# A two-layer kernel with a GRU scan: input and constant loads by need, one gate product in front of the last weight turn, and the recurrence with its routing and output two steps sooner in the loop

## What is computed

```
proj  = attention over 8 block sums of x (keys Wk, query cond, softmax) through Wo
x     = x + FFN(layernorm(x + proj) * gamma + beta)          # layer 0
        FFN: silu(gate) * up, then down; 512 -> 2048 -> 512,
        activations and weights quantised in blocks of 32 (shared exponent)
h_t   = GRU(h_{t-1}, x_t), h_0 = cond, t = 0 .. 255           # layer 1
        r = sigmoid(i_r + h_r); z = sigmoid(i_z + h_z)
        n = tanh(i_n + r * h_n); h_t = (1 - z) * n + z * h_{t-1}
route = silu(h @ rw1.T + rb1) @ rw2.T + rb2 + gates           # top 2 of 16 experts
x     = x + h @ W.T + bias + sum over the 2 experts of rank-16 products
```

## Time and profile before

| | before |
|---|---|
| time, median of 3 runs | 1708.49 us (1707.1 to 1712.42) |
| the profiled execution's own time | 1712.84 us |
| its span | 1711.0 us |
| PE, PEld busy | 1551.7 us (91%), 1198.1 us (70%) |
| DVE, ACT, POOL busy | 1399.7 us (82%), 644.3 us (38%), 496.8 us (29%) |
| mean granted PE clock | 0.963 |
| first and last start of the r and n products | 226.87 us, 1691.36 us |

### The profile page before, as it was taken

How to read it: one execution, slowest core, us unless ns; L and a number is a source line. 1 busy time by engine, 2 the same in 40 slices (tenths; PEclk the granted TensorE clock), 3 DMA queues, 4 the chain that set the end, 5 groups by cost and what they waited for, 6 DMA issues and landing times.

```text
span 1711.0 us, 75109 instructions
## 1 busy us (share of the span) xinstructions
PE 1551.7 (91%) x32268; PEld 1198.1 (70%) x32268; DVE 1399.7 (82%) x5571; ACT 644.3 (38%) x1624; POOL 496.8 (29%) x573
## 2 busy tenths in 40 slices
PE   5633689999999999999999999999999999999986
PEld 2321367777777777777777777777777777778874
DVE  7787888888888888888888888888888888887654
ACT  5666243333333333333333333333333333333331
POOL 6774322222222222222222222222222222221000
PEclk9866699999999999999999999999999999999998
DMA  7744211112211111122111112212111212211000
GB/s 245 267 154 135 57 45 43 42 47 49 49 46 49 31 40 49 46 46 50 48 41 49 49 46 49 37 35 47 46 46 49 49 43 46 49 43 37 25 15 20
DMA packets 122444, 101.01 MB, mean 59 GB/s; under 512 B 91904, under 2 KB 92288, under 8 KB 121728
## 3 DMA queue, kind: packets, MB, share of 16 engines
q1 hardware_dynamic: 121824, 96.02, 21.1%
q10 hardware_dynamic: 288, 0.19, 0.0%
HBM read 58.43 MB, written 16.78 MB: 44 GB/s over the span
## 4 chain that ended last, share of the span: by engine, by line
PE 77%; DVE 14%; issue 3%; DMA 2%; POOL 2%; ACT 2%; SPq 0%; DVEq 0%; ACTq 0%; POOLq 0%
PE ps_rn_turn L1311 25%; PE ps_gi L1212 12%; PE ps_z L1311 10%; PE ps_down L1179 6%; PE ps_gate_up L1170 6%; PE ps_gate_up L1160 4%; PE ps_base L1221 4%; PE ps_base L1264 3%; PE ps_route L1221 3%; DVE fe L821 1%; POOL qfT L1028 1%; DVE gi L630 1%; DVE gi L628 1%; DVE hT L808 1%; PE ps_rn_turn L1200 1%
## 5 line engine op out<-in xcount | busy, mean ns | idle before, releaser
L1311 PEld LDWEIGHTS ps_rn_turn<-hT,whh 128*128 128x128 f16 x16320 | 435.0, 96 | 86.0 <-DVE hT L759 72.2
L1311 PE MATMUL ps_rn_turn<-hT,whh 128*128 128x32 f16 x16320 | 449.3, 177 | 46.1 <-DVE hT L759 45.4
L1046 POOL TENSOR_TENSOR qf<-f8c,fe 128x512 bf16<-128x512 bf16 x128 | 134.1, 1047 | 862.1 <-DVE f8c L838 862.1
L583 ACT ACTIVATE r_tanh<-r_pre,scale_half 128x64 f32<-128x64 f32 x256 | 89.0, 348 | 563.5 <-DVE r_pre L779 563.5
L1212 PEld LDWEIGHTS ps_gi<-x1T,wih 128*128 128x128 f16 x4608 | 270.6, 98 | 32.8 <-issue 3.1
L1212 PE MATMUL ps_gi<-x1T,wih 128*128 128x128 f16 x4608 | 289.3, 220 | 1.6 <-ACT gi L574 1.6
L1311 PE MATMUL ps_z<-hT,whh 128*128 128x32 f16 x8160 | 243.3, 177 | 0.0
L1311 PEld LDWEIGHTS ps_z<-hT,whh 128*128 128x128 f16 x8160 | 222.6, 96 | 0.0
L574 ACT ACTIVATE gi<-ps_gi,b_i,scale_x 128x128 f32<-128x128 f32 x384 | 144.4, 456 | 196.7 <-PE ps_gi L1212 196.7
L773 DVE TENSOR_TENSOR r_half<-ps_rn_turn,gi 128x64 f32<-128x64 f32 x256 | 57.2, 224 | 149.9 <-PE ps_rn_turn L1311 146.1
L585 ACT ACTIVATE z_tanh<-z_pre,scale_half 128x64 f32<-128x64 f32 x256 | 89.0, 348 | 157.0 <-DVE z_pre L789 157.0
(11 more groups left out here) (201 smaller groups left out, 2408.5 us busy)
## 6 DMA issues: line engine op xcount, KB each, us to landing
wih<-in_x_steps SPq DMA_DIRECT2D x32, 256.0 KB, 5.4
xin<-in_x_steps SPq DMA_DIRECT2D x32, 256.0 KB, 2.9
...
```

Of the source, the lines that this page charges most:

```text
L583: nc.scalar.activation(r_tanh[:, :], r_pre[:, :], ACT.Tanh, scale=HALF_S_INV).then_inc(r_ok, 1)
L1046: g.tensor_tensor(blocked(qf[:, :]), blocked(f8c[:, :]), spread(fe16[:, :]), ALU.mult).then_inc(qf_done, 1)
L1311: last = mm(ps[:, (at + j) * 2 * B:(at + j + 1) * 2 * B], whh[:, k, u, gate * D + j * P:gate * D + (j + 1) * P], hx(t)[:, 2 * k:2 * k + 2, ...
```

## The change

- **x and constants.** Block sums take 8 tiles in piece 0 and the rest over the next 9 (`sums_upto`; `SUM_PARTS` 10, so that hops and slots come two pieces sooner: `FIRST_HOP` 9, `FIRST_SLOT` 19). SP issues x one piece ahead of its sums, the first 8 tiles behind two weight pieces. The four constants of the attention come at pieces 7 and 8, the others at 14 to 18. The slots of c = -4 stand beside pieces 19 to 23, the last four of them before piece 23.
- **Gate product.** PE's `gate(0, 0)` is issued in front of the turn of piece 23; DVE's first `scales` in front of a constant's cast; the sum of the biases moves from an attention hop to `gru_weights`.
- **Two steps sooner** (`AHEAD`). R and L no longer go by s but by b: tile r and step b are those of c * 8 + s + 2. What was done in slot s for b = s now stands two slots sooner: b = 0 in slot 6 and 1 in slot 7 of the iteration before, b = 2 to 7 in slots 0 to 5. The loads of x1 and the stores of y go with them. Q, F, E and I stay where they were. `x_parts` end one slot sooner, ACT's `gi` moves from slots 1, 3, 5 to 1, 2, 4, and the `base` parts spread over b = 0, 1, 2, 6.

```diff
 XRING = 8
-SUM_PARTS = 12
+SUM_PARTS = 10
 ATTENTION = 10
 FIRST_HOP = SUM_PARTS - 1
 FIRST_SLOT = FIRST_HOP + ATTENTION
...
-FILL_UPS = 11
+FILL_UPS = 10
+AHEAD = 2
...
+def beside_piece(p):
+    if p < PIECES - 1:
+        return range(max(p - FIRST_SLOT, 0), max(p - FIRST_SLOT + 1, 0))
+    return range(p - FIRST_SLOT, STEPS)
+def sums_upto(p):
+    return 0 if p < 0 else min(TILES, XRING + p * (TILES - XRING) // (SUM_PARTS - 1))
...
-    return tuple(0 <= c + d < TILES for d in (4, 3, 2, 1, 0, -1))
+    return tuple(0 <= c + d < TILES for d in (4, 3, 2, 1))
+def recurrent(c, s):
+    r, b = divmod(c * STEPS + s + AHEAD, STEPS)
+    return r, b, 0 <= r < TILES, 0 <= r - 1 < TILES
...
-        if p < 0:
-            return 0
-        return min(TILES, max(min(p + 1, 2) * XRING // 2, (p - 1) * TILES // SUM_PARTS))
+        return sums_upto(p - 1)
...
-        if 8 <= p < 8 + (CONSTS + 1) // 2:
-            for dst, src in small[(p - 8) * 2:(p - 7) * 2]:
-                sp.dma_start(dst, src).then_inc(consts if p > 8 else att_consts, 16)
+        if p in (7, 8):
+            for dst, src in small[(p - 7) * 2:(p - 6) * 2]:
+                sp.dma_start(dst, src).then_inc(att_consts, 16)
+        if 14 <= p < 19:
+            for dst, src in small[(p - 12) * 2:(p - 11) * 2]:
+                sp.dma_start(dst, src).then_inc(consts, 16)
         if p == SUM_PARTS + 1:
             sp.dma_start(wk_sb, WkT).then_inc(wkwo_loaded, 16)
         if p == SUM_PARTS + 3:
...
         if 0 <= k < KD:
             sp.wait_ge(at_pe, 2)
             sp.dma_start(wih[:, k, :], W_hh[:, k, :]).then_inc(whh_loaded, 16)
-        if p >= FIRST_SLOT:
-            slot(-4, p - FIRST_SLOT)
+        for s in beside_piece(p):
+            slot(-4, s)
+    def load_x1(l):
+        wait(sp, x1b_done, count(l, 1))
+        sp.wait_ge(x1_stored, count(l, 1, 1) * 16)
+        sp.dma_start(x1_in[:, :], rows(x1_dram, l)).then_inc(x1in_loaded, 16)
+    def store_y(l):
+        sp.wait_ge(y_ok, count(l, 1, 1))
+        sp.dma_start(rows(out, l), y[:, :]).then_inc(y_stored, 16)
...
+        r, b, R, L = recurrent(c, s)
         turns(c, s)
         if s == 0:
             loads(c)
+        if L and b == 0:
+            load_x1(r - 1)
+        if L and b == STEPS - 1:
+            store_y(r - 1)
         if s == 4 and c + 5 < TILES:
...
-        if I and s in (1, 3, 5):
+        if I and s in (1, 2, 4):
...
-        if p >= PIECES - KD:
+        k = p - PIECES + KD + 1
+        if 0 <= k < KD:
             act.wait_ge(whh_loaded, 16 * KD)
-            absolute_sums(0, p - PIECES + KD, wih[:, p - PIECES + KD, :])
-    for s in range(STEPS):
-        slot(-4, s)
+            absolute_sums(0, k, wih[:, k, :])
     over_tiles(slot)
...
-            dve.wait_ge(consts, 16 * (CONSTS - 2))
-            v.tensor_tensor(b_i[:, 0:2 * KD], b_i[:, 0:2 * KD], b_h[:, 0:2 * KD], ALU.add).then_inc(c_dve, 1)
...
         if s == 3:
+            dve.wait_ge(consts, 16 * (CONSTS - 4))
+            v.tensor_tensor(b_i[:, 0:2 * KD], b_i[:, 0:2 * KD], b_h[:, 0:2 * KD], ALU.add).then_inc(c_dve, 1)
...
-        if L and here == (6, 0):
+        if L and there == (6, 0):
...
-            recur(c, s, beside)
+            recur(r, b, beside)
...
+    scales(0, 0)
     dve.wait_ge(first_consts, 32)
     v.tensor_copy(idb[:, :], idf[:, :]).then_inc(c_dve, 1)
-    scales(0, 0)
     scales(0, 1)
     scales(1, 0)
     for p in range(PIECES):
-        if p >= FIRST_SLOT:
-            slot(-4, p - FIRST_SLOT)
+        for s in beside_piece(p):
+            slot(-4, s)
...
+            if q == 0:
+                pool.wait_ge(consts, 16 * (CONSTS - 4))
...
-        if L and s == 3:
+        if L and b == 3:
...
-        for t in range(p * TILES // SUM_PARTS, min((p + 1) * TILES // SUM_PARTS, TILES)):
+        for t in range(sums_upto(p - 1), sums_upto(p)):
...
     def max_row(e, L):
         pe.wait_ge(x_small, count(e, 6, 2))
+        wait(pe, x_scale_ok, count(e, 1))
         if L:
-            pe.wait_ge(l_small, count(e - 3, 6, 1))
+            pe.wait_ge(wxaT_ok, count(e - 3, 1, 1))
...
-            pe.wait_ge(wxaT_ok, count(e - 3, 1, 1))
+            pe.wait_ge(xa_ok, count(e - 2, 1, 1))
...
-            wait(pe, x_scale_ok, count(l + 2, 1, 1))
+            wait(pe, x_small, count(l + 2, 6, 3))
...
+        pe.wait_ge(x_scale_ok, count(l + 2, 1, 1))
         turn_(ps_h1T, hid[:, :], idf[:, :]).then_inc(hidT_mm, 1)
...
-    def turn_wxa(l, E):
+    def turn_wxa(l):
         pe.wait_ge(wxa_ok, count(l, 1, 1))
-        if E:
-            pe.wait_ge(x_small, count(l + 3, 6, 3))
...
-    x_parts = ((0, (0,)), (0, (1, 2, 3)), (1, (0, 1)), (1, (2, 3)), (2, (0, 1)), (2, (2, 3)))
-    base_parts = {4: (0,), 6: (1, 2, 3)}
+    x_parts = ((0, (0, 1)), (0, (2, 3)), (1, (0, 1, 2, 3)), (2, (0, 1)), (2, (2, 3)))
+    base_parts = {0: (0,), 1: (1,), 2: (2,), 6: (3,)}
     base_parts_at_end = {0: (0,), 3: (1, 2, 3)}
...
-        if F:
+        if F and (f, s) != (0, 0):
             (gate, up)[s % 2](f, s // 2)
...
+        if (r, b) == (0, 0):
+            pe.wait_ge(inter_done, FILL_UPS)
         if R:
-            pe.wait_ge(hx_ok, c * STEPS + (s + 1))
-            t = c * STEPS + s - 1
+            pe.wait_ge(hx_ok, r * STEPS + (b + 1))
+            t = r * STEPS + b - 1
...
     for p in range(PIECES):
         block_sums(p)
         attention(p - FIRST_HOP)
+        if p == PIECES - 1:
+            pe.wait_ge(w_ev, PIECES - 1)
+            gate(0, 0)
         piece(p // 2, p % 2)
-    for s in range(STEPS):
-        slot(-4, s)
     pe.wait_ge(w_ev, PIECES)
```

More of the change, by code:

```diff
@@ L358, in beside @@
                     sp.dma_start(wih[:, k, :], W_hh[:, k, :]).then_inc(whh_loaded, 16)
-                if p >= FIRST_SLOT:
-                    slot(-4, p - FIRST_SLOT)
-            def loads(c):
[L363 to L367, removed]
+                for s in beside_piece(p):
[7 more added lines that the diff above has]
+                sp.dma_start(rows(out, l), y[:, :]).then_inc(y_stored, 16)
+            def loads(c):
+                Q, F, E, I = stages(c)
                 if E:
@@ L862, in ffn, with others @@
                         clip(f8c, f8, f8_done, at, qf_done, f8c_done)
-            def others(c, s, place, Q, F, E, I, L):
-                q, e, i, l = c + 4, c + 2, c + 1, c - 1
+            def others(c, s, place, Q, F, E, I, r, b, L):
+                q, e, i, l = c + 4, c + 2, c + 1, r - 1
                 ffn(c, s, place, F, E)
-                here = (s, place)
-                if L and here == (1, 0):
+                here, there = (s, place), (b, place)
+                if L and there == (1, 0):
                     dve.wait_ge(xa_ok, count(l, 1, 1))
@@ L886, in others @@
                     v.tensor_tensor(gap[:, :], top[:, 0:1], top[:, 1:2], ALU.subtract).then_inc(l_small, 1)
-                if L and here == (5, 2):
+                if L and there == (5, 2):
                     dve.wait_ge(l_small, count(l, 6, 5))
                     v.tensor_copy(at_f[:, :], top_at[:, :]).then_inc(l_small, 1)
-                if L and here == (6, 0):
+                if L and there == (6, 0):
                     dve.wait_ge(coeff_ok, count(l, 3, 3))
@@ L946, in others @@
                     clip(q8c, q8, q8_done, count(q, 1), qx_done, q8c_done)
-                if L and here == (7, 3):
+                if L and there == (7, 3):
                     dve.wait_ge(y_mm, count(l, 1, 1))
@@ L1062, in slot @@
                     g.tensor_tensor(x1_bias[:, :], x1_in[:, :], bias_b[:, :], ALU.add).then_inc(x1b_done, 1)
-                if L and s == 5:
+                if L and b == 5:
                     pool.wait_ge(gap_ok, count(l, 1, 1))
@@ L1084, in _ @@
                 piece(p // 2, p % 2)
-            for s in range(PIECES - FIRST_SLOT, STEPS):
-                slot(-4, s)
             over_tiles(slot)
@@ L1301, in others @@
                 if L:
-                    for k in (base_parts if R else base_parts_at_end).get(s, ()):
+                    for k in (base_parts if R else base_parts_at_end).get(b, ()):
                         base(l, k)
```

77 lines of the change are left out of this document (36 added, 41 removed).

## The result

The changed kernel takes **1699.19 us** (median of 5 runs, 1696.14 to 1700.55) against 1709.12 for the kernel before (5 runs, 1707.1 to 1712.42). The ratio is .9926, 95% interval .991 to .9942: faster by .6 to .9%, clear of noise. Forecast were 1699.8, and 1678 to 1718. The profiled execution took 1696.49 us and its span is 1694.6 us, 16.4 less than the span of before (1711.0). A second profiled execution of this kernel has a span of 1697.7, so some 3 us of the 16.4 belong to one execution. The medians differ by 9.9 us and the ratio stands for some 12.6, so the 16.4 overstates the gain: the profiled execution of before took 1712.84, more than any of the five.

What follows compares the result with a forecast made beforehand. PE's work was taken to bound the loop, with a smaller part from the recurrence's chain. Terms -9.8 + 6.0 - 6.4 - 2.5 + 4.0 = -8.7 us, off 1708.49, gave 1699.8 us; range 1678 to 1718.

Steps and rivals of the forecast that it cites:

- steady loop: 27 repeated tiles: slots sum to 46.67 us against 46.52, +.15 per tile, +4.0 us in all.
- The end and the start of the recurrence: Two bare steps fall away at the end, -9.8 us; slots 6 and 7 of iteration -1 take them, +6.0.
- The prologue: Before the first products: DMA waits on weight pieces -6.4 us, ACT's wait for W_ih -2.5.
- the two longest: Prologue: DVE's longest DMA waits on the two buffers' weight pieces are saved, -6.4 us; bounds 0 and -11.2.
- L612's waits near 5 in all: Sign in the prologue: near 5 us of DMA waits would show the forecast right, still near 11 wrong.
- The gate at 0: Prologue: gate group ahead of the last turn costs PE .86 but starts the FFN sooner; net 0, bounds -.9 and +.9.
- Slot 2: Steady tile: second xg ends 4.43 behind the products, 2.4 left, so 6.83 us against PE's 5.97; bounds 5.97 and 7.17.
- Slot 1: Steady tile: x_in_bias meets rn or n_pre and holds it, 5.98 us; bounds PE's 5.88 and 6.3.
- rival B: POOL holds nothing on the path: slots 1 and 2 are PE's, tile 45.71, -22 us in the loop, 1674; chance .10.
- Slot 4: Steady tile: wxa, .61, enters DVE's work ahead of r_half, .2 leaves: 5.85 us; bounds 5.49 and 6.04.
- C: Rival: POOL's ops hold the chain for all their length in slots 1, 2, 4; tile 47.52, 1722.8 us; chance .15.
- D: Rival: prologue DMA waits only move, all 8.9 us come back elsewhere; 1708.7 us, no change; chance .20.

Runs made afterwards that it cites:

- e8: The changed kernel with all 13 constants from piece 7 on, two per piece, beside the x tiles: 1699.88 us, ratio .9942 to the kernel before.
- e3: The changed kernel with POOL's x_in_bias moved from slot 1 to slot 5: 1675.88 us, ratio .9797 to the kernel before.
- e4: The changed kernel with DVE's xn op at the head of its work in slot 2, before inter and fam: 1670.11 us, ratio .9753 to the kernel before.
- e10: The changed kernel with x_in_bias back in slot 3, its place before the change: 1698.8 us, ratio .9925 to the kernel before.

## Why the prediction was right, point by point

The time was 1699.2 for 1699.8. The direction was right for the reasons given at the edges and in the prologue. That the number agrees to .6 us is in part luck. The steady loop was forecast to cost 4.0 us and gained 4.5, and by the two spans the whole gained 16.4 and 13.4 where the sum of the terms was 8.7: the terms' errors don't cancel there. The ratio's gain is some 12.6 us and the medians' 9.9; the base of the forecast, 1708.49, was .6 under the later median of before.

- **The end and the start of the recurrence.** -8.7 and +6.4 for -9.8 and +6.0, the second within its bounds, the first 1.1 off. The two steps in slots 6 and 7 took 5.05 and 5.32; the chain bounds them, as said. From iteration 31 to the last products 10.5 us were saved, and what follows them takes 1.8 back: from the last r and n products to the end 21.5 us against 19.7. That tail was a term put at nothing.
- **The prologue.** -9.2 in this trace, -6.9 in the second one, -7.2 by itself, for -8.9. The size was about right, the split only in part. "I take the two longest as saved, 4.6 + 1.8": the 4.6 did go (.6 is left, at 67.27). The 1.8 went at piece 1 and came back at piece 2, where the wait rose from 2.2 to 4.7 behind eight x tiles. In all DVE waited 4.6 us less for DMA where 6.4 were taken (6.0 less in the second execution), and the last piece came 4.3 sooner. The sign that I had named, L612's waits near 5 in all, was a bad one, since after the change that line also has the start's wait of 5.3. With the constants back at piece 7 (e8) the waits behind piece 2 are 4.9 in all, for 1.5 in the trace beside it. ACT's 3.2 for W_ih are gone (2.5 taken). The gate at 0 held: undone together with the slots' order it cost nothing. Where the other 4.9 of the 9.2 come from, between the last piece and the first products, stays open; in the second execution they are 2.2.
- **Slot 2** was 6.82 for 6.83. Here the step that shifted `xg` by PE's lost lateness held: the second `xg` ends 4.50 behind the products for 4.43, and 2.32 are left for 2.4. That two ops would be held, .83 and 1.26, the forecast didn't say; it needed only the end of `xg`. e3 and e4 show it as cause: each takes one of its two conditions away, and each takes the slot to 6.10 or below.
- **Slot 1** was 5.89 for 5.98. `rn` was held 1.20, as the upper bound had it, and PE's work covered it with nothing to spare. But pricing each slot by its own hold, as the forecast and rival B did, was a step that failed without showing in the sum: the hold in slot 1 is a condition of that in slot 2 (e3, -.72 there). The price of slot 2 came out right since I had taken the lateness of PE there as gone; I hadn't seen that `x_in_bias` was what made it go.
- **Slot 4** was 5.57 for 5.85, the largest mis-sized term of the loop, -.28 per tile or 7.6 of the 8.5 us by which iterations 1 to 27 beat the forecast. I took `wxa` at .61. In slot 4 no op of POOL stands beside it, and it takes .42:

```profile
L914 DVE TENSOR_TENSOR wxa<-xa,coeff 128x256 f32<-128x256 f32 x32 | 13.3, 416 | 4.5 <-POOL coeff L1097 4.5
```

  The .61 was a mean of mostly held ops (.65 in the steady part): in slot 6 of before POOL's `qx` ran beside it. So `r_half` starts 2.05 behind the products and not near 2.2, and PE is busy for all of the slot's 5.58.
- **Rivals.** B's tile of 45.7 is what e3 measures (45.59), once one op is elsewhere; as a reading of the change it was wrong, both holds are there. C's upper bounds came in none of the three slots. D was wrong in the time. Waits did move, from piece 1 to 2 and from the constant's cast to the first piece, and L612's waits, D's sign, stayed over 11; but 4.6 us of waiting for DMA vanished.
- **On the Trainium skill's rule** of the exclusive port pair (page "SBUF — State Buffer", section "SBUF: two separate sides"): the trace agrees. `rn` (1.20), `fe` (.83, 1.26) and `gap` (.96, in e10) all end within .1 of the POOL op that was there first. The forecast set the rule's 5.98 for slot 1 against PE's 5.88 by the shorter holds of the rows, 2.7 us of the sum. The hold came as the rule says, and PE's work hid it: the time of slot 1 is that of the other reading, 5.89. That reading's sum, 2.7 us lower, left out that slot 2 changes with slot 1.
